# Softmax denominators in an attention kernel: every second key tile summed by an adding transfer, in place of two in five

## The reference

```
scores = einsum('bhqd,bhkd->bhqk', qh, kh) * scale
mask   = arange(Lkv)[None, :] <= arange(Lq)[:, None]
attn   = softmax(where(mask, scores, -inf), axis=-1)
out    = einsum('bhqk,bhkd->bhqd', attn, vh)
```

## Time and profile before

| | |
|---|---|
| median of 3 runs | 2974.31 us (2970.31 to 2976.27) |
| the profiled execution, span from first to last instruction | 2975.9 us |
| PE busy | 2870.5 us (96%) |
| DVE busy | 1851.0 us (62%) |
| POOL busy | 1572.6 us (53%) |
| ACT busy | 1520.9 us (51%) |
| q0, the queue of POOL's transfers, of 16 engines | 25.8% |
| `attend` in the profile | from about 288 us to 2095 us |

### The profile page before, as it was taken

One profiled execution on the slowest core, in us unless ns is written; L12 is line 12 of the kernel. 1 busy time (PEld: TensorE's weight loads), 2 busy tenths in 40 slices (PEclk: granted clock), 3 DMA queues, 4 the chain that ended last, 5 costly groups with the idle time before them and its releaser, 6 DMA issues. The chain is left out here.

```text
span 2975.9 us, 42860 instructions
## 1 busy us (share of the span) xinstructions
PE 2870.5 (96%) x15944; PEld 1701.8 (57%) x15944; DVE 1851.0 (62%) x3452; ACT 1520.9 (51%) x2896; POOL 1572.6 (53%) x656
## 2 busy tenths in 40 slices
PE   8999999999999999999999999989889999999996
PEld 7876555555555554555554555543676666655664
DVE  4466888876688775788775787741653443344434
ACT  3232456666566666565676565666234333344332
POOL 0000367889577899567899567896751110111110
PEclk9998999999999999999999999999899999999998
DMA  6568445558545558544568443566692110011000
GB/s 244 184 205 233 122 112 121 129 118 191 141 112 117 128 127 194 141 112 106 128 140 191 123 104 99 135 147 144 216 299 71 43 43 28 16 43 43 29 29 15
DMA packets 133990, 366.26 MB, mean 123 GB/s; under 512 B 12032, under 2 KB 28928, under 8 KB 112288
## 3 DMA queue, kind: packets, MB, share of 16 engines
q0 software_dynamic: 26512, 184.83, 25.8%
q1 hardware_dynamic: 102096, 169.34, 19.9%
q10 hardware_dynamic: 5184, 9.44, 0.9%
HBM read 114.59 MB, written 70.78 MB: 62 GB/s over the span
## 5 line engine op out<-in xcount | busy, mean ns | idle before, releaser
L1046 ACT ACTIVATE pT<-s_bank 128x512 f32<-128x512 f32 (+5 forms) x2176 | 1086.6, 578 | 665.3 <-PE s_bank L1215 472.9
L1063 DVE TENSOR_REDUCE row_max<-m_bank 128x1 f32<-128x512 f32 (+4 forms) x2240 | 1252.4, 622 | 268.1 <-PE m_bank L1168 172.9
L986 POOL TENSOR_TENSOR part_sum<-part_sum,pT 128x2048 f32<-128x2048 f32 x231 | 1092.4, 4729 | 81.7 <-ACT pT L1046 74.2
L1215 PE MATMUL s_bank<-q_sb,k_sb 104*128 104x512 f32 (+3 forms) x2176 | 839.3, 411 | 26.5 <-ACT pT L1046 20.8
L1168 PE MATMUL m_bank<-k_sb,q_sb 96*128 96x512 f32 (+4 forms) x2240 | 839.7, 408 | 8.7 <-POOL max_terms L958 2.5
L1168 PEld LDWEIGHTS m_bank<-k_sb,q_sb 96*128 96x128 f32 x2240 | 429.1, 194 | 206.4 <-DVE row_max L1063 129.3
L1215 PEld LDWEIGHTS s_bank<-q_sb,k_sb 104*128 104x128 f32 x2176 | 411.1, 192 | 221.6 <-ACT pT L1046 137.0
L1232 PE MATMUL o_bank<-pT,v_sb 128*32 128x512 f32 (+5 forms) x4352 | 499.6, 576 | 0.0
L1640 POOL TENSOR_TENSOR f_var_eps<-f_mean_var,eps 128x4 f32<-128x4 f32 x8 | 1.6, 201 | 484.4 <-DVE f_mean_var L1813 484.4
L986 POOL TENSOR_TENSOR part_sum<-pT 128x2048 f32<-128x2048 f32 x28 | 127.7, 4560 | 235.0 <-ACT pT L1046 194.1
L1232 PEld LDWEIGHTS o_bank<-pT,v_sb 128*32 128x32 f32 (+1 forms) x4352 | 113.3, 109 | 228.9 <-ACT pT L1046 114.8
(11 more groups left out here) (195 smaller groups left out, 3481.6 us busy)
## 6 DMA issues: line engine op xcount, KB each, us to landing
moved_sum<-pT POOLq DMA_DIRECT2D x168, 1024.0 KB, 7.2
q_sb<-qT_hi SPq DMA_DIRECT2D x64, 256.0 KB, 5.2
k_sb<-kT_hi SPq DMA_DIRECT2D x48, 256.0 KB, 7.4
x_in<-in_x SPq DMA_DIRECT2D x8, 1024.0 KB, 6.1
qT_hi<-q_hi SPq DMA_DIRECT2D x8, 1024.0 KB, 4.2
qT_lo<-q_lo SPq DMA_DIRECT2D x8, 1024.0 KB, 6.5
q_sb<-qT_lo SPq DMA_DIRECT2D x32, 256.0 KB, 4.8
aT<-o_sb ACTq DMA_DIRECT2D x32, 256.0 KB, 5.8
```

The lines of the kernel that those rows point to most:

```text
L986: pool.tensor_tensor(total, pT[:, slot(S - 1), :, q0:] if j and kt == 1 else total, pT[:, slot(S), :, q0:], ALU.add).then_inc(pool_added, 1)
L1046: act.activation(pT[0:rows, slot(S), h, q0:], s_bank[(HG * S + h) % S_RING][0:rows, q0:], ACT.Exp, scale=SCALE).then_inc(exp_done, 1)
L1063: dve.tensor_reduce(row_max[:, j % 2, r, h, c:c + 1], m_bank[p % M_BANKS][:, 0:n], AX_X, ALU.max).then_inc(unit_max, 1)
L1215: mm = pe.matmul(out[:, q0:], k_sb[0:R_END, h, at:at + P], q_sb[query_buffer(g, j)][0:R_END, h, q0:], start=True, stop=kt < 4 * j)
```

## The change

```diff
--- before
+++ after
@@ -501,7 +501,7 @@ def adder(j, kt):
     if kt > 4 * j or kt == KT - 1:
         return "matmul"
-    return "transfer" if j and kt % 5 in (2, 4) and kt <= key_tiles(j) - 4 else "pool"
+    return "transfer" if j and kt and kt % 2 == 0 and kt <= key_tiles(j) - 4 else "pool"
```

## The result

| | before | changed |
|---|---|---|
| median | 2972.31 us (4 runs) | 2960.07 us (2959.7 to 2962.7, 4 runs) |
| span of the profiled execution | 2975.9 us | 2961.1 us |
| ratio | | 0.9947, 95% interval 0.9934 to 0.996 |

The forecast of 2986.5 us had the wrong sign, and 2960.07 lies just under the range of 2962 to 3004. The first rival said 2959 to 2966. (2960.07 by 2975.7 is 0.9947.)

A forecast was written before the change was run, and what follows sets the result against it. PE, busy for 2870.5 of 2975.9 us, was taken as the bound. 31.2 us lost to added transfers against 13.5 + 5.4 gained made 12.3 us slower: span 2988.2, median predicted 2986.5 us, range 2962 to 3004.

The forecast's parts named there:

- first rival: The DMA engines have room after all and the kernel gets faster, 2959 to 2966 us, say 2963; chance 0.26.
- What bounds the kernel: PE sets the pace; its time changes only where it stands still or runs at a lower clock.
- three places: Block 6, block 7 of groups 0 to 2 with POOL and DMA full, and the last block with its stalls.
- POOL's side: POOL works 148 us less; gains of 13.5 us in the last block and 5.4 at block 6's end.
- the last block: Last block of the kernel: stalls behind late transfers go, 13.5 us gained, bounds 7 and 15.
- the end of block 6 in groups 1 and 2: PE's idle time and slowed matmuls around tile 22 go: 2.7 us, twice, 5.4 gained; bounds 2 and 7.
- The DMA side: Block 7 of groups 0 to 2: two more adding transfers cost 10.4 us a group, 31.2 lost in all.
- the room before the crowd: Block 7 of groups 0 to 2: free DMA share 0.18 of 10 us, taking up 1.8 us of transfers.
- the crowd behind: After block 7: late transfers run into the next group's first loads, 2 us a group charged.
- second rival: The next group's loads in block 7 take the delay, some 5 us a group lost; 2971 us, chance 0.15.
- What would show it: Signs: frequent ACT waits, landings past 12 us, block 7 growing 5 to 10 us, POOL's busy time down 150 to 180.

The follow-up runs named there:

- x_lower: The kernel before with the new pattern (every second tile moved) only in blocks 2 to 5 of all groups; 0.9998 of the kernel before.
- x_last: The kernel before with the new pattern only in blocks 6 and 7 of the last group; 0.9966 of the kernel before, 10 us faster.
- x_crowd: The kernel before with the new pattern only in blocks 6 and 7 of groups 0 to 2; 0.9988 of the kernel before, 3.6 us faster.
- x_skip: The changed kernel with its ten extra transfers in each group left out, their tiles summed by nobody; 0.9949 of the kernel before.
- x_slow1: The changed kernel with one small addition of constants on POOL ahead of each of the 208 transfers; 0.9976 of the kernel before.
- x_third: The changed kernel with two key tiles in three moved in blocks 6 and 7 of groups 0 to 2; 1.0141 of the kernel before.
- x_plus1: The changed kernel with one transfer more, tile 13, in block 7 of groups 0 to 2; 1.0019 of the kernel before.

## Why the prediction was wrong

**What bounds the kernel: right.** The three places were the right ones, and blocks 2 to 5 gave nothing (x_lower, within 3 us).

**POOL's side: right in kind, near in size.** 13.5 us were taken for the last block; 10 came (x_last, and the same from the two timelines). The stalls went; what the sum missed are two lowered clocks of PE, 1.1 and 1.4 us over 5.50, and 0.80 us that PE still stands before the last denominators. For the end of block 6 in groups 1 and 2 I had 5.4, twice the row of group 2; in group 1 the idle time was 1.64 us and the 16 matmuls took 2.68, so that both together were 4.8. There the 16 matmuls are back at 1.92 us, and block 7 shrank by 6.8 us over the three groups; by the times it is 3.6 (x_crowd). A pair of steps takes POOL 5.14 us and not 5.47: the next addition starts 0.6 us after an issue, whose 0.88 us overlap it. The experiments with POOL's load confirm the cause beyond the timelines: half the gain goes with 0.29 us more of POOL a step.

**The DMA side: this is the step that failed.** "Two are 10.8 us. They can use the room before the crowd [...] So 8.4 us of transfers come too late", and with the crowd behind 31.2 in all. Measured: nothing for all 40 added transfers, within some 5 us (x_skip), and 3.6 us gained in these blocks (x_crowd). Two things were wrong in it, and they are parts of the first two rivals.

The room was taken from a share of 1.00. But the packets' times add up to a full share at 209 GB/s as well as at 234, so the stretches had room: in the middle one 1.3 MB in 60 us, half of it in the 10 us ahead of the crowd, for which I had counted 1.8 us. Before, POOL gave out its transfers in twos, 5.2 us apart and then 10.5, being busy for 59.4 of 60 us:

```profile
1148.23 0.85 POOL L972 DMA_DIRECT2D moved_sum<-pT  x1
...
1153.39 1.16 POOL L972 DMA_DIRECT2D moved_sum<-pT  x1
...
1163.86 0.87 POOL L972 DMA_DIRECT2D moved_sum<-pT  x1
```

My reading, which no run isolates, is that the engines were crowded after such a pair and less so before the next, and that waiting in the crowd was booked as busy time. That POOL was busy doesn't by itself hold the rate down, as x_slow1 shows, where the transfers are evenly spaced and there is one in two steps.

The same page of the Trainium skill that I had weighed (DMA: Bandwidth & Descriptors, "Queues, rings and completion order") says that each engine takes turns between the queues packet by packet. The trace doesn't contradict that, and no run isolates it. It would fit the loads' giving way: a packet of the transfers' queue holds some 7 KB (9.33 MB in 1283 packets), one of the loads' queue 1 KB (4.26 MB in 4339), so that with equal turns the transfers would get most of the bytes.

And I had written off the loads: "while ACT stands, the next loads, which follow PE's steps, stand too". True if ACT stands. It hardly did (5.4 us in the three blocks together, 7.6 before), and the loads gave way: 0.75 MB of them left the stretch, landing 11 to 16 us after their issue in the median, and nobody waits for the next group's keys in this block. The second rival had this, and I had put it at 15%. The measured time is the first rival's, 2959 to 2966 at 26%, but that its number fits is partly luck: it took 9 us as lost and 18.9 as gained, where nothing measurable was lost and 14 to 16 gained.

Beyond the eleventh transfer of a block one costs 6 to 7 us, near the 5.4 that I had charged. That this is the same price isn't shown: I had charged busy time of the DMA engines, and what the runs measure there holds the wait in the chain and PE's lowered clock as well. What they do show is that the mistake was a linear price from the first added transfer on; the cost begins between the eleventh and the twelfth, where the twelfth is put between two others.

**What would show it** named the signs well: ACT was to wait often in block 7, landings were to pass 12 us. The slowest did pass (13.9; 11.8 in the median of the middle stretch), and ACT's waits fell all the same. POOL's busy time fell by 146 us, a little less than the 150 to 180 named there.

## What to carry to other kernels

A DMA share near 1.0 doesn't say that the engines are full: look at the bytes moved at that share, in several stretches, and take the highest rate seen as the ceiling before charging an added transfer for it. Ask of each queue in the crowd who waits for it and how long it can be put off; the slack of the queue that nobody waits for comes before any stall. And an engine at 99% of a stretch that issues transfers in its own stream makes them late; a unit of work moved off it can be worth more than it costs, until the next limit, which here came with one transfer more, put between two others.

## What the runs showed of the hardware

An adding transfer of 1 MB within SBUF lands 6.9 to 7.0 us after its issue where hardly anything else moves (issues at 2036.12 and 2067.47 us of the kernel before), a copying one after 4.4 to 4.6. A mix of adding transfers and loads moved 228 to 238 GB/s in the 60 us stretches with a share over 1.02 of the changed kernel, x_third and x_plus1, and no stretch of theirs more; in the kernel before, a stretch with a share of 1.03 moved 209. PE's granted clock fell twice in the last block of the changed kernel, to a mean of 0.61 of full from 2008 to 2011 us and of 0.60 from 2031 to 2035, so mostly the lower of its two levels (1.2 for 2.4 GHz), in turns with no idle time over 0.31 us; what set it off stays open. So does why block 7 of group 2 is still 3.5 us longer than that of group 1.
